# Two layers of gated cross-attention and routed experts: another way to list the tokens, another order of gathers and sums, another row order in memory

## The reference

```
x = x + tanh(g_xattn[0]) * attention(layernorm(x), context)   # 16 heads of 8
x = x + tanh(g_ffn[0])   * experts_1(layernorm(x))            # 8 experts, one per token, hidden 256
x = x + tanh(g_xattn[1]) * attention(layernorm(x), context)   # 16 heads of 8
x = x + tanh(g_ffn[1])   * experts_2(layernorm(x))            # 8 experts, two per token, hidden 512
```

## Time and profile before

| what | value |
|---|---|
| median of 3 runs | 759.71 us (758.35 to 764.55) |
| the profiled execution's own time | 760.45 us |
| its span in the trace | 758.6 us |
| PE busy | 539.6 us (71%) |
| DVE busy | 502.7 us (66%) |
| ACT busy | 358.3 us (47%) |
| POOL busy | 315.0 us (42%), DMA issues of 0.95 us each among it |
| moved by the DMA queues | 74.50 MB, mean 98 GB/s |

### The profile page before, as it was taken

One profiled execution on the slowest core, in us unless ns is written; L12 is line 12 of the kernel. 1 busy time (PEld: TensorE's weight loads), 2 busy tenths in 40 slices (PEclk: granted clock), 3 DMA queues, 4 the chain that ended last, 5 costly groups with the idle time before them and its releaser, 6 DMA issues.

```text
span 758.6 us, 16969 instructions
## 1 busy us (share of the span) xinstructions
PE 539.6 (71%) x5534; PEld 435.7 (57%) x5534; DVE 502.7 (66%) x1605; ACT 358.3 (47%) x830; POOL 315.0 (42%) x439
## 2 busy tenths in 40 slices
PE   0699999998721039872699988888403999999940
PEld 0466777776510028761466756665302999999940
DVE  5568888887358862222699999998561556655625
ACT  0246777776633014330167766677402555555510
POOL 6212222221200057743755227456772455555440
PEclk9959999999955558996599999999755999999985
DMA  8443334332000004362556546241123222222229
GB/s 262 153 136 92 101 109 115 107 88 66 16 14 1 0 21 97 99 84 66 146 163 185 163 135 190 84 121 53 40 64 101 61 69 71 79 72 72 65 70 296
DMA packets 100532, 74.50 MB, mean 98 GB/s; under 512 B 12928, under 2 KB 94592, under 8 KB 100160
## 3 DMA queue, kind: packets, MB, share of 16 engines
q1 hardware_dynamic: 92336, 55.17, 25.5%
q0 software_dynamic: 7040, 14.56, 7.6%
q10 hardware_dynamic: 1072, 3.70, 1.4%
HBM read 43.64 MB, written 31.39 MB: 99 GB/s over the span
## 4 chain that ended last, share of the span: by engine, by line
PE 41%; DVE 22%; issue 11%; POOL 10%; DMA 8%; ACT 5%; SPq 2%; ACTq 1%; POOLq 0%; DVEq 0%
PE bank L943 10%; PE bank L953 10%; DVE MX L1089 7%; PE bank L740 5%; POOL PT L582 5%; PE bank L766 4%; PE bank L887 4%; PE bank L754 3%; POOL dispatched L556 3%; DVE PT L1285 2%; DMA PT<-normed,LIST 2%; PE bank L842 1%; ACT XT_HL_WR L654 1%; DMA QS_N<-MH 1%; ACT OT L678 1%
## 5 line engine op out<-in xcount | busy, mean ns | idle before, releaser
L623 ACT ACTIVATE PT<-bank 128x512 f32<-128x512 f32 x256 | 151.8, 597 | 95.1 <-PE bank L754 93.9
L1089 DVE TENSOR_REDUCE MX<-bank 128x4 f32<-128x512 f32 x256 | 172.1, 681 | 25.9 <-PE bank L766 24.2
L766 PE MATMUL bank<-KS,QS_N 96*128 96x128 f16 x1024 | 104.5, 228 | 16.7 <-DVE MX L1089 8.7
L593 POOL DMA_INDIRECT returned<-PT,META_ROW x78 | 74.9, 961 | 84.6 <-DVE PT L1403 72.4
L953 PEld LDWEIGHTS bank<-WALL,HT 128*128 128x128 f32 x808 | 100.9, 194 | 5.1 <-issue 1.7
L953 PE MATMUL bank<-WALL,HT 128*128 x808 | 102.1, 278 | 0.6 <-issue 0.6
L943 PE MATMUL bank<-XGT,XT_HL_WR 128*128 128x256 f32 x404 | 101.9, 392 | 0.0
L766 PEld LDWEIGHTS bank<-KS,QS_N 96*128 96x128 f16 x1024 | 76.6, 103 | 43.4 <-DVE MX L1089 15.3
L754 PE MATMUL bank<-QS_N,KS 98*128 98x512 f16 x256 | 98.0, 388 | 1.8 <-DMA QS_N<-MH 1.6
L943 PEld LDWEIGHTS bank<-XGT,XT_HL_WR 128*128 128x128 f32 x404 | 75.0, 198 | 8.0
L556 POOL DMA_INDIRECT dispatched<-N,SLOT x64 | 64.3, 1004 | 30.0 <-issue 14.1
(11 more groups left out here) (210 smaller groups left out, 917.4 us busy)
## 6 DMA issues: line engine op xcount, KB each, us to landing
spread<-XT_HL_WR SPq DMA_DIRECT2D x96, 128.0 KB, 2.0
QS_N<-spread SPq DMA_DIRECT2D x128, 48.0 KB
KS<-spread SPq DMA_DIRECT2D x32, 192.0 KB
PT<-dispatched SPq DMA_DIRECT2D x39, 132.0 KB, 2.1
WALL<-in_w SPq DMA_DIRECT2D x8, 578.0 KB
CT<-in_ctx SPq DMA_DIRECT2D x32, 128.0 KB
returned<-PT SPq DMA_DIRECT2D x23, 128.0 KB, 2.2
WALL<-in_w ACTq DMA_DIRECT2D x1, 2048.0 KB, 8.5
```

The lines of the kernel that those rows point to most:

```text
L593: pool.indirect_dma_start(ys[1][:, :], bass.IndirectOffsetOnAxis(ap=META_ROW[:, a.f, c:c + 1], axis=0), YS[:, a.f, c, :], None).then_inc(S ...
L623: nc.scalar.activation(PT[:, c, 4 * g:4 * g + 4, :].rearrange("p j q -> p (j q)"), ST[i % 2][:, :], ACT.Exp, scale=SCALE[layer]).then_inc( ...
L766: last = nc.tensor.matmul(MB[i % 2][:, j * P:(j + 1) * P], QS[0:96, m.r, J * g + j, c * P:(c + 1) * P], KS[0:96, m.r, g, c * P:(c + 1) * P ...
L1089: V.tensor_reduce(out=MX[:, m.u, 2 * J * g + c:2 * J * (g + 1):2], in_=MB[i % 2][:, :].rearrange("p (j k) -> p j k", j=J), op=ALU.max, axi ...
```

## The change

The list: DVE cuts a tile number, a block (2 x tile plus the place's lowest bit) and a position (the next 7 bits). A single number per token, its row minus 2048, is multiplied onto `OWN` by DVE itself, in float16; ACT and POOL take no part. `POS` is float16 too and is compared in steps of 12, 8, 8 and 4 batches. PE sums 46 columns, and one DVE instruction adds 2048. A place without a token gets 2048.

The results of layer 1: pairs 0 and 1 are gathered ahead of the slots, the others by the table `GATHERS`; the sums are made by the table `SUMS_AT`, which names slot and step.

The rows: the token of batch b on partition p has row 32 p + b in `normed` and `ys[1]`, and place s of a tile sits on partition s >> 1 of it.

```
+PARTS = (0, 12, 20, 28, 32)
+GATHERS = {-4: (2, 3), -3: (4, 5), -2: (6, 7, 8), -1: (9, 10, 11), 0: (12, 13, 14), 1: (15,)}
+SUMS_AT = {(-4, 0): 0, (-3, 0): 1, (-2, 0): 2, (-2, 5): 3, (-1, 0): 4, (-1, 2): 5, (-1, 5): 6, (0, 1): 7, (0, 3): 8, (0, 4): 9, (0, 6): 10,
+           (1, 1): 11, (1, 2): 12, (1, 4): 13, (1, 6): 14, (2, 1): 15}
...
-    tokens = (np.arange(B)[None, :] * P + p).astype(np.int32)
-    rows = np.concatenate([tokens, tokens + T], axis=1).astype(np.int32)
+    rows = (B * p + np.arange(B)[None, :]).astype(np.int32)
...
-                    sp.dma_start(normed[y.b * P:(y.b + 2) * P, :].rearrange("(c p) d -> p c d", p=P),
+                    sp.dma_start(normed.rearrange("(p b) d -> p b d", b=B)[:, y.b:y.b + 2, :],
...
-                    sp.dma_start(ys[0][i * TILE:(i + 1) * TILE, :].rearrange("(c p) d -> p c d", p=P), YS[:, a.f, :, :]).then_inc(SO[a.f], 16)
+                    sp.dma_start(ys[0][i * TILE:(i + 1) * TILE, :].rearrange("(p c) d -> p c d", c=2), YS[:, a.f, :, :]).then_inc(SO[a.f], 16)
...
-                    y = ys[1].rearrange("(b p) d -> p b d", p=P)
-                    sp.dma_start(N[:, b, 0:D], y[:, B + 8 * k:B + 8 * k + 8, :]).then_inc(YL[k], 16)
-                    sp.dma_start(N2[:, b, 0:D], y[:, b, :]).then_inc(YL[k], 16)
+                    first, second = (ys[1][T * c:T * (c + 1), :].rearrange("(p b) d -> p b d", b=B) for c in range(2))
+                    sp.dma_start(N[:, b, 0:D], second[:, b, :]).then_inc(YL[k], 16)
+                    sp.dma_start(N2[:, b, 0:D], first[:, b, :]).then_inc(YL[k], 16)
...
-                        for k in range(2 * p + 9, min(2 * p + 11, PAIRS)):
+                        for k in GATHERS[p] if p in GATHERS else ():
                             gather_results(Pair(1, k // 4, k % 4))
...
-                pool.wait_ge(own, 1)
-                nc.gpsimd.tensor_tensor(out=IDS[:, :, 1, :], in0=OWN[:, :, :], in1=const("batch").unsqueeze(2).broadcast_to([P, B, BLOCKS]),
-                                        op=ALU.mult).then_inc(ids_b, 1)
...
-                gather_results(Pair(1, 0, 0))
+                for k in range(2):
+                    gather_results(Pair(1, 0, k))
...
-                    act.wait_ge(own, 1)
-                    nc.scalar.activation(IDS[:, :, 0, :], OWN[:, :, :], ACT.Copy, scale=const("partition")).then_inc(ids_p, 1)
...
-                    pe.wait_ge(ids_p, 1)
-                    pe.wait_ge(ids_b, 1)
+                    pe.wait_ge(ids, 1)
                     for b in range(B):
-                        if b % (B // 4) == 0:
-                            pe.wait_ge(positions, 4 * b // B + 1)
-                        last = nc.tensor.matmul(PA[:, 0:2 * BLOCKS], POS[:, b, :], IDS[:, b, :, :].rearrange("p k n -> p (k n)"),
-                                                start=(b == 0), stop=(b == B - 1))
+                        if b in PARTS:
+                            pe.wait_ge(positions, PARTS.index(b) + 1)
+                        last = nc.tensor.matmul(PA[:, 0:BLOCKS], POS[:, b, :], IDS[:, b, :], start=(b == 0), stop=(b == B - 1))
...
+                    def add_result(u):
+                        if layer == 1 and (p, u) in SUMS_AT:
+                            k = SUMS_AT[p, u]
+                            k = Pair(1, k // 4, k % 4)
+                            dve.wait_ge(YGS[k.p % 8], 32 * (k.p // 8 + 1))
+                            for c in range(2):
+                                last = V.scalar_tensor_tensor(out=batch(k, c), in0=YG[:, k.p % 8, c, :], scalar=W0[:, k.b + c:k.b + c + 1],
+                                                              in1=batch(k, c), op0=ALU.mult, op1=ALU.add)
+                            last.then_inc(combined, 1)
...
                     routing(0)
-                    if n and layer == 1:
-                        dve.wait_ge(YGS[n.p % 8], 32 * (n.p // 8 + 1))
...
+                    add_result(0)
                     maxima(1)
                     if n:
+                        if layer == 1:
+                            dve.wait_ge(combined, n.p + 1)
...
-                link(V.tensor_scalar(out=block, in0=SLOT[:, 0, :], scalar1=7, scalar2=None, op0=ALU.arith_shift_right))
-                link(V.tensor_scalar(out=place, in0=SLOT[:, 0, :], scalar1=P - 1, scalar2=None, op0=ALU.bitwise_and))
-                link(V.tensor_copy(SM[:, 4:6, :], CUT[:, :, :]))
...
+                link(V.tensor_scalar(out=tile, in0=slots, scalar1=7, scalar2=-2, op0=ALU.arith_shift_right, op1=ALU.bitwise_and))
+                link(V.tensor_scalar(out=block, in0=slots, scalar1=1, scalar2=None, op0=ALU.bitwise_and))
+                link(V.tensor_tensor(out=block, in0=block, in1=tile, op=ALU.bitwise_or))
+                link(V.tensor_scalar(out=place, in0=slots, scalar1=1, scalar2=P - 1, op0=ALU.arith_shift_right, op1=ALU.bitwise_and))
+                link(V.tensor_copy(SM[:, 4:6, :], CUT[:, 0:2, :]))
+                link(V.tensor_tensor(out=OWN[:, :, :], in0=const("blocks").unsqueeze(1).broadcast_to([P, B, BLOCKS]),
+                                     in1=sm[4].unsqueeze(2).broadcast_to([P, B, BLOCKS]), op=ALU.is_equal))
+                V.tensor_tensor(out=IDS[:, :, :], in0=OWN[:, :, :], in1=const("row_less_half").unsqueeze(2).broadcast_to([P, B, BLOCKS]),
+                                op=ALU.mult).then_inc(ids, 1)
+                for part in range(len(PARTS) - 1):
+                    b = slice(PARTS[part], PARTS[part + 1])
+                    n = PARTS[part + 1] - PARTS[part]
+                    V.tensor_tensor(out=POS[:, b, :], in0=const("places").unsqueeze(1).broadcast_to([P, n, P]),
+                                    in1=sm[5][:, b].unsqueeze(2).broadcast_to([P, n, P]), op=ALU.is_equal).then_inc(positions, 1)
...
-                link(V.tensor_copy(FIRST_IDS[:, :], PA[:, 0:BLOCKS]))
-                V.scalar_tensor_tensor(out=LIST[:, :], in0=PA[:, BLOCKS:2 * BLOCKS], scalar=float(P), in1=FIRST_IDS[:, :],
-                                       op0=ALU.mult, op1=ALU.add).then_inc(list_ready, 1)
+                V.tensor_scalar(out=LIST[:, :], in0=PA[:, 0:BLOCKS], scalar1=float(T // 2), scalar2=None, op0=ALU.add).then_inc(list_ready, 1)
```

More of the change, by code:

```diff
@@ L88, in constants @@
         ("blocks", one * np.arange(BLOCKS)[None, :]),
-        ("batch", one * np.arange(B)[None, :]),
-        ("partition", one * p),
+        ("row_less_half", B * p + np.arange(B)[None, :] - T // 2),
         ("search_sign", one * sign),
@@ L201, in program @@
         SAME = sb("SAME", [P, P], BF16)
-        ROWS = sb("ROWS", [P, 2 * B], I32)
+        ROWS = sb("ROWS", [P, B], I32)
         WALL = sb("WALL", [P, E * max(WCOLS)])
@@ L299, in program @@
          n_kept, lg_done, lg_kept, dve_own, pool_own, act_own, set_dve, set_pool, shifted, exp_e, lows_cut, lows_ready, candidates, counted_act,
-         mask_ready, own, ids_p, ids_b, positions, listed, list_ready, normed_kept, counted, ranked, tables_ready, scattered, pads, xg0, xg1, xg2, w_loaded, w_kept, meta,
+         mask_ready, ids, positions, listed, list_ready, normed_kept, counted, ranked, tables_ready, scattered, pads, xg0, xg1, xg2, w_loaded, w_kept, meta,
          xg_t, xg_kept, h_done, gelu_done, y_done, y_kept, sc0, sc1, sc2, sc3, yl0, yl1, yl2, yl3, xa0, xa1, xa2, so0, so1, so2, so3, yg0, yg1, yg2, yg3, yg4, yg5, yg6, yg7, combined, stored,
@@ L306, in program @@
             n_stats n_rstd n_copied n_t n_kept lg_done lg_kept dve_own pool_own act_own set_dve set_pool
-            shifted exp_e lows_cut lows_ready candidates counted_act mask_ready own ids_p ids_b positions listed list_ready normed_kept counted ranked tables_ready scattered pads xg0 xg1 xg2 w_loaded w_kept
+            shifted exp_e lows_cut lows_ready candidates counted_act mask_ready ids positions listed list_ready normed_kept counted ranked tables_ready scattered pads xg0 xg1 xg2 w_loaded w_kept
             meta xg_t xg_kept h_done gelu_done y_done y_kept sc0 sc1 sc2 sc3 yl0 yl1 yl2 yl3 xa0 xa1 xa2 so0 so1 so2 so3 yg0 yg1 yg2 yg3 yg4 yg5 yg6 yg7 combined stored settled
@@ L1101, in slot @@
                     routing(0)
-                    if n and layer == 1:
-                        dve.wait_ge(YGS[n.p % 8], 32 * (n.p // 8 + 1))
-                        for c in range(2):
-                            last = V.scalar_tensor_tensor(out=batch(n, c), in0=YG[:, n.p % 8, c, :], scalar=W0[:, n.b + c:n.b + c + 1],
-                                                          in1=batch(n, c), op0=ALU.mult, op1=ALU.add)
-                        last.then_inc(combined, 1)
-                        dve.wait_ge(combined, n.p + 1)
+                    add_result(0)
                     maxima(1)
                     if n:
+                        if layer == 1:
+                            dve.wait_ge(combined, n.p + 1)
                         dve.wait_ge(x_norm, before(n.g - 1))
@@ L1114, in slot @@
                     routing(1)
+                    add_result(1)
```

(19 more changed lines are left out.)

7 lines of the change are left out of this document (3 added, 4 removed).

## The result

The change made the kernel a little faster: median 757.4 us (754.02 to 760.1, 20 runs) against 759.49 (757.52 to 764.55, 20 runs). The ratio is 0.9966, 95% interval 0.9952 to 0.998, so 2.6 us by the ratio, 1.5 to 3.6 by its interval. Measured once more beside other kernels it was 0.9959 (0.9941 to 0.9977). The profiled execution took 757.23 us with a span of 755.4. The forecast was 757.2 with a range of 753 to 762.

What follows compares the result with a forecast made beforehand. DVE was taken to bound both attention stages, with POOL filling layer 2's first slots. 760.45 - 0.9 (list) - 0.1 (stores) + 0.5 (gathers and sums) - 2.0 (tail) = 757.95, less 0.74 for the median: 757.2 us, range 753 to 762.

Steps and rivals of the forecast that it cites:

- term 4: Layer 2's slots, moved sums: pair 6 5.2 us late, later slots shorter; together +0.5 us, bounds -1.5 and +3.
- the tail: Last reads after the slots: half become 4 KB runs, 400 instead of 296 GB/s; -2.0 us, bounds 0 and -3.6.
- The list: Listing of layer 1's tokens: one product on DVE replaces POOL's and ACT's; 10.74 us becomes 9.80, so -0.9 us.
- The store: Layer 1's results stored in 128 rows of 1 KB instead of 256 of 512 B; -0.1 us, bounds 0 and -0.2.
- The gathers: Start of layer 2: four gathers ahead hidden, slot -3 gains 0.4 us, six gathers in slot -2 make pair 3 +2.1.
- 4 x 0.63 = +2.5: Layer 2, between normalisations of pairs 4 and 5: five sums instead of one while DVE is full, +2.5 us.
- six of them route and are DVE's alone: 6 x 0.63 = -3.8: Layer 2's later slots: six that route tokens lose a sum each and shorten by its full time, -3.8 us.
- routing slots shorter by less than 0.6: Sign of being wrong: layer 2's slots that route tokens do not get shorter by 0.6 us.
- The three balanced slots: Layer 2's slots of 9.50 us with PE at 9.06: losing their sums gives half, -0.9 us, bounds 0 and -1.9.
- The rival of 16 KB between rows: Layer 1's tile gathers slow down because consecutive tokens lie 16 KB apart; +27 us, 784 us, chance 0.10.
- The rival of a tail without gain: Last reads: the queues are bound by something row length does not change; 759.2 us, chance 0.17.
- the best case: Rival: tail gains 3.6 us, balanced slots gain in full, ramp without its two 0.3; 754.8 or 754.0 us, chance 0.20.

Runs made afterwards that it cites:

- e3: The changed kernel with the list made by two numbers again (ACT and POOL multiply, four equal comparisons, 92 columns); 758.29 us, 0.9981 of the kernel before.
- e9: The kernel before, unchanged, run once more for its profile; median 759.53 us, its one profiled execution 761.91 us.
- e4: The changed kernel with places without a token reading different rows, with three more small DVE operations on the list; 754.12 us, 0.9929 of the kernel before.
- e2: The changed kernel with gathers and sums of layer 1's results in the old order (pair 0 ahead, two pairs per slot, one sum per slot); 755.41 us, 0.9952.
- e11: The changed kernel with two pairs of gathers per slot instead of up to three, later sums one per slot; 754.57 us, 0.993 of the kernel before.
- e1: The changed kernel with rows numbered 128 b + p again, new places and 1 KB stores kept; 757.75 us, 0.9982 of the kernel before.

## Why the prediction was right

The total was right to 0.2 us. That is in good part luck: inside term 4 two errors of 1.6 to 2 us cancelled, and the tail missed by half a us.

1. **The list**: -0.9 forecast, -0.96 measured in every profile. POOL's product as what slowed a comparison is shown by e3; the prediction read it as the first comparison, and it is the second (3.66 us, before as in e3), which leaves the sum as it was. The unseen product of DVE was priced by its like of equal size and cost just that.
2. **The store**: -0.1 forecast; the stage is 70.8 to 71.3 us in six profiles with the new places against 71.47 in e9, so -0.1 to -0.6. No run took the stores back by themselves, so that this is their doing is not shown. The first profile's 1.7 us more were mostly a single late gather (e9). In the same stage lay 3.4 us that neither kernel took, though the earlier trace rows showed them and I used the row only as a price: the reads of one row (e4).
3. **The gathers**: the ones ahead hidden, as forecast. Pair 3: +2.1 forecast, +1.6 to +2.0 measured, and undone by e2 and e11 alike. POOL without idle time is the mechanism, shown in the rows above; the two gathers more cost 2.35 us in slot -2 (8.70 us for 6.35 between its variance and the next), and slot -3 had won 0.7 and not 0.4.
4. **The sums**: forecast pair 6 5.2 late and 4.7 given back. The cleanest comparison is e1, e3 and e4 against e2, which has the old order on the new list and whose clock did not fall either: pair 6 is 3.2 to 3.3 us late, 3.0 to 3.2 are given back by pair 15, and 0.1 to 0.4 remain of the +0.5 forecast.
   - Late: the term "4 x 0.63 = +2.5" between pairs 4 and 5 measured +1.9, the stretch from 5 to 6 became shorter by 0.6 instead of longer by 0.3. In the changed kernel's own two profiles, where the clock fell, pair 6 is 3.2 to 5.7 us late against the two profiles before.
   - Given back: the term "six of them route and are DVE's alone: 6 x 0.63 = -3.8" was mis-sized. Against the kernel before, pair 9 to pair 15 went from 64.55 to 61.63 us, -2.9 or 0.49 a slot; three slots gave 0.66 to 0.71, two 0.4 to 0.5, and the one from pair 9 to 10 nothing: DVE's work in it fell from 10.10 to 9.83 us and its length did not, so it was not DVE's alone (the two windows above). The prediction named routing slots shorter by less than 0.6 as a sign that it is wrong; on their mean this part was. Moreover e2, with its sums in the old places, needs 63.86 us there, so 0.7 of the 2.9 is not the order's; where it comes from is open. The three balanced slots gave 0.75 of the 0.9.
   - In all, pair 15 came at 147.0 and 145.7 in the changed kernel against 144.9 and 146.3 before, and at 144.5 to 144.8 in the three relatives. The order is worth nothing within that scatter. What it wins in the later slots it spends before pair 6.
5. **The tail**: -2.0 forecast, 22.6 to 21.05, -1.55 measured, shown by e1. The rate while reading became 346 GB/s, where 296 and 400 for the two halves make 340, so that was near. The missing half us: the forecast took the faster rate for all 4.19 MB, but the first of the four steps landed no sooner (5.7 and 5.8 us after the first read). For the three steps behind it, 3.15 MB at 346 instead of 296 GB/s are 1.54 us less, what DVE's pauses lost.

With the measured sizes, -0.96 for the list, -0.3 for the stage of the stores and -1.5 for the tail, the sum is -2.8 without the order, and the ratio gives -2.6 (-1.5 to -3.6): the order's own share is not told apart from nothing by it. The rival of 16 KB between rows (0.10) is refuted: a tile's two gathers are issued 2.5 us apart as before and the stage did not grow. The rival of a tail without gain (0.17) is refuted by 346 GB/s and by e1. Of the best case (0.20), the tail's 3.6 us and the balanced slots in full did not come true; of the ramp, the two times 0.3 us between pairs 3 and 4 and 5 and 6 stayed away where the clock did not fall (e3: 8.65 us for 8.61 before, and 9.34 for 9.56).

What stays open: how much the old order is faster. By the ratios e2 is 1.1 us under the changed kernel and e11 2.2; each interval overlaps that of the changed kernel, and both point the same way; where the clock did not fall, the stages give e2 only 0.1 to 0.4 us at pair 15. A fall of the clock between pairs 4 and 5 adds 0.9 to 2.0 us with the five sums there and 0.8 with one. It came in two of five profiles of either kind, which is too few to say whether the new order makes it more frequent.

## What to carry to other kernels

Work moved out of full slots into the filling of a pipeline is also paid for by whatever engine issues its inputs: count that engine's instructions in the stretch before the sums on the one that is relieved. Move no more than keeps that engine ahead; here two pairs of gathers per slot brought pair 3 2.2 us sooner than three (25.2 for 27.4), and the kernel's median was 2.4 us lower, part of which the sums' places may have made. And a row of the profile that is used as a price, busy queues that move little, should be asked what it costs itself.
